# Local attention on one core: transposed product with the values, probabilities scaled by VectorE and GpSimd

## The reference, cut to what matters

```python
qkv = shift_token(x) @ wqkv                  # 128 -> 3 x 512
q, k = l2norm(q) * qs, l2norm(k) * ksc       # per head
q, k = rotary_xpos(q, k)
sim = einsum('bhwid,bhwjd->bhwij', 8.0 * bq, look_around(bk))   # 64 x 128 per window
attn = softmax(where(mask, -max, sim))
x = x + (attn @ look_around(bv)) @ wo
h = layer_norm(shift_token(x)) * lg + lb
a, g = split(h @ w1 + b1)                    # 341 each
x = x + (a * gelu(g)) @ w2 + b2
```

## Time and profile before

| | us |
|---|---|
| runs: median (lowest to highest of 3) | 1923.7 (1919.97 to 1941.29) |
| profiled execution: its own time | 1931.87 |
| profiled execution: span | 1930.0 |
| stage windows(0), tiles in flight | about 330 to 720 |
| stage windows(1), tiles in flight | about 1075 to 1475 |
| TensorE busy in the span | 1632.6 |

### The profile page before, as it was taken

How to read it: one execution, slowest core, us unless ns; L and a number is a source line. 1 busy time by engine, 2 the same in 40 slices (tenths; PEclk the granted TensorE clock), 3 DMA queues, 4 the chain that set the end, 5 groups by cost and what they waited for, 6 DMA issues and landing times. The chain is left out here.

```text
span 1930.0 us, 38058 instructions
## 1 busy us (share of the span) xinstructions
PE 1632.6 (85%) x13334; PEld 1162.4 (60%) x13334; DVE 1219.7 (63%) x3746; ACT 1071.4 (56%) x2763; POOL 905.9 (47%) x668
## 2 busy tenths in 40 slices
PE   5999996899999977899888689999976675959777
PEld 4999995566666643344555366666654554637655
DVE  3555554887777754555754688777745985646465
ACT  3655553778888834566433478888862112325332
POOL 1333333776667612223443677666623674441044
PEclk9999998999999986889756799999998896979889
DMA  5000000111111100000000011111100001110012
GB/s 208 1 1 1 1 1 4 29 33 26 32 27 26 26 6 1 1 1 1 2 1 1 20 29 26 33 28 26 32 15 1 1 1 33 23 33 1 15 30 23
DMA packets 41082, 38.64 MB, mean 20 GB/s; under 512 B 21944, under 2 KB 32192, under 8 KB 40512
## 3 DMA queue, kind: packets, MB, share of 16 engines
q1 hardware_dynamic: 35264, 32.02, 6.4%
q0 software_dynamic: 5632, 4.20, 1.8%
HBM read 13.14 MB, written 4.20 MB: 9 GB/s over the span
## 5 line engine op out<-in xcount | busy, mean ns | idle before, releaser
L979 ACT ACTIVATE arena<-ps 128x512 f32<-128x512 f32 (+5 forms) x680 | 358.2, 581 | 301.1 <-PE ps L327 98.4
L1218 ACT ACTIVATE arena<-ps 128x320 f32<-128x320 f32 (+4 forms) x256 | 131.9, 561 | 153.3 <-PE ps L686 152.3
L1135 ACT ACTIVATE arena<-arena,g_small 128x128 f32<-128x128 f32 x512 | 198.7, 406 | 0.5
L2194 POOL TENSOR_TENSOR arena<-arena,consts 128x512 f32<-128x512 f32 (+1 forms) x64 | 93.0, 1454 | 209.8 <-ACT arena L1218 209.8
L1676 DVE CUSTOM_DVE_ANT_0 arena<-ps,consts,g_ss 128x128 f32<-128x128 f32 x512 | 145.6, 347 | 58.5 <-PE ps L521 58.5
L2234 POOL TENSOR_TENSOR arena<-arena 128x512 f32<-128x512 f32 x64 | 81.9, 1280 | 176.1 <-DVE arena L1684 176.1
L686 PE MATMUL ps<-arena 32*128 32x160 f32 (+4 forms) x1024 | 129.6, 505 | 18.8 <-ACT arena L1218 9.0
L327 PE MATMUL ps<-consts,arena 128*128 128x128 f32 x400 | 81.7, 341 | 59.6 <-DVE arena L1651 11.3
L686 PEld LDWEIGHTS ps<-arena 32*128 32x128 f32 x1024 | 65.8, 232 | 91.4 <-ACT arena L1218 51.9
L1683 DVE TENSOR_TENSOR arena<-ps,tabs 128x512 f32<-128x512 f32 x128 | 87.8, 686 | 52.3 <-ACT arena L1104 45.6
L327 PEld LDWEIGHTS ps<-consts,arena 128*128 128x128 f32 x400 | 55.2, 172 | 100.3 <-DVE arena L1474 20.4
(11 more groups left out here) (257 smaller groups left out, 4180.2 us busy)
## 6 DMA issues: line engine op xcount, KB each, us to landing
arena<-arena SPq DMA_DIRECT2D x112, 128.0 KB, 2.3
weights<-in_w SPq DMA_DIRECT2D x1, 5069.0 KB, 24.3
weights<-in_w SPq DMA_DIRECT2D x1, 2052.0 KB, 12.8
arena<-Y SPq DMA_DIRECT2D x64, 32.0 KB
arena<-Y SPq DMA_DIRECT2D x64, 31.8 KB
consts<-in_c SPq DMA_DIRECT2D x1, 1278.0 KB, 8.7
sorted_rows<-X SPq DMA_DIRECT2D x1, 1024.0 KB, 5.1
X<-sorted_rows SPq DMA_DIRECT2D x4, 256.0 KB, 3.9
```

Of the source, the lines that this page charges most:

```text
L979: copy = lambda o, i: act.activation(o, i, ACT.Copy)
L1135: last = act.activation(g_p[:, n % 2, 4 * hf + i, :], g_sc[:, 4 * hf + i, :], ACT.Exp, scale=-1.0, bias=g_mn[:, h:h + 1], accum_out=g_rs[: ...
L1218: act.activation(b_p[:, U % 2, 2 * gp:2 * gp + 2, at:at + n], ps[:, b:b + 2, 0:n], ACT.Exp, scale=float(HD) ** -0.5).then_inc(s.b_exp, 1)
L2194: pool.tensor_tensor(v, v, m.unsqueeze(1).broadcast_to([P, NG, n]), ALU.mult)\
```

## The change

- `values`: the operands change places. The values are stationary, the transposed probabilities move, and the result comes out transposed (rows are head columns). `turn_out`, its semaphore and the buffer `g_os` go; `keep_out` copies bank 3 instead of bank 2, at the start of the step instead of after `keep_qk`.
- The division by the sums moves ahead of the transposes: VectorE scales the four even heads' probabilities in place (`scale_even`, last in step n), GpSimd the four odd heads' (`scale_odd`, in step n of its loop between the keys' scaling and the queries' root, released by a reciprocal that VectorE makes in step n+1 between the two halves of `minima`). `turn_probs` waits for these instead of for `exps`.
- TensorE's order in a step: `out_rows` where `turn_out` was; `project_v` before `values`.
- VectorE's order: `add_out` between `rope_k` and `rope_q`; `mid` before `sums`; statistics of the feed-forward part at lag 6 instead of 7. `root4(1)` on GpSimd at lag 6 too.
- ScalarE: `gelu` at lag 10 after `keep_qk`, not at lag 9 at the step's end.
- SyncE: `shift(t - 2)` before `lookback(t + 2)`.

```diff
@@ -558,7 +557,7 @@
         N = n0 + n
-        pe.wait_ge(gs.exp, 2 * N + hf + 1)
+        pe.wait_ge(gs.odd if hf else gs.even, N + 1)
         pe.wait_ge(gs.kin if hf else gs.qin, n0 + tiles_by(t + 1))
@@ -572,36 +571,30 @@
         pe.wait_ge(vx_sem[j], (32 if j else 16) * (N // NT + 1))
-        need(pe, gs.os, N)
+        need(pe, gs.oin, N)
         need(pe, gs.hin, m0 + groups_by(t, -3))
         need(pe, gs.y, m0 + groups_by(t, 12))
-        for h in range(HF):
+        for i in range(4):
             for r in range(2):
-                src = g_v if r else g_vx
-                last = mm(ps[64 * r:64 * r + 64, 3, h * DF:(h + 1) * DF],
-                          g_pT[:, 4 * (h % 2) + h // 2, 64 * r:64 * r + 64],
-                          src[:, j, h * DF:(h + 1) * DF], start=True, stop=True, skip_group_check=True)
+                for hf in range(2):
+                    h, src = 2 * i + hf, g_v if r else g_vx
+                    last = mm(ps[64 * hf:64 * hf + 64, 3, i * P + 64 * r:i * P + 64 * r + 64],
+                              src[:, j, h * DF:(h + 1) * DF], g_pT[:, 4 * hf + i, 64 * r:64 * r + 64],
+                              start=True, stop=True, skip_group_check=True)
         last.then_inc(gs.pv, 1)
-
-    def turn_out(n):
-        N = n0 + n
-        pe.wait_ge(gs.os, N + 1)
-        pe.wait_ge(gs.vin, n0 + tiles_by(n + 3))
-        need(pe, gs.add, N)
-        for c in range(4):
-            last = tr(ps[:, 2, c * P:(c + 1) * P], g_os[:, c * P:(c + 1) * P], ident)
-        last.then_inc(gs.ot, 1)
...
         pe.wait_ge(gs.oin, N + 1)
+        pe.wait_ge(gs.vin, n0 + tiles_by(n + 3))
+        need(pe, gs.add, N)
         for c in range(4):
...
     def turn_y(g, t):
-        need(pe, gs.os, n0 + tiles_by(t - 2))
+        need(pe, gs.oin, n0 + tiles_by(t - 2))
         need(pe, gs.hin, m0 + g)
@@ -645,7 +638,7 @@
         if live(t - 2):
-            turn_out(t - 2)
+            out_rows(t - 2)
         if at_step(t, 10):
@@ -659,12 +652,10 @@
                 up((t - lag) // 4, c, half, t)
-        if live(t - 2):
-            out_rows(t - 2)
+        if live(t + 2):
+            project_v(t + 2, t)
         if live(t - 1):
             values(t - 1, t)
-        if live(t + 2):
-            project_v(t + 2, t)
         if at_step(t, 7):
@@ -1122,9 +1113,9 @@
         N = n0 + n
-        act.wait_ge(gs.ot, N + 1)
+        act.wait_ge(gs.pv, N + 1)
         need(act, gs.out, N)
-        copy(g_oT, ps[:, 2, :].rearrange("p (c t) -> p c t", c=4)).then_inc(gs.oin, 1)
+        copy(g_oT, ps[:, 3, :].rearrange("p (c t) -> p c t", c=4)).then_inc(gs.oin, 1)
@@ -1171,12 +1162,14 @@
     for t in range(-4, TILES + 9):
+        if live(t - 2):
+            keep_out(t - 2)
         if live(t + 2):
...
             keep_qk(t + 1)
-        if live(t - 2):
-            keep_out(t - 2)
+        if at_step(t, 10):
+            gelu((t - 10) // 4)
         if live(t - 1):
@@ -1193,8 +1186,6 @@
             keep_hn((t - 7) // 4)
-        if at_step(t, 9):
-            gelu((t - 9) // 4)
         for i in {34: (1, 3), 36: (7,), 39: (13,)}.get(t, ()) if F == 0 else ():
@@ -1659,12 +1650,22 @@
     heads = lambda t: t.rearrange("p (h d) -> p h d", h=HF)
-
-    def norm_out(n):
+    halves = lambda t: t.rearrange("p (i f) -> p f i", f=2)
+
+    def reciprocals(n, hf):
         N = n0 + n
-        dve.wait_ge(gs.pv, N + 1)
-        need(dve, gs.ot, N)
-        tt(heads(g_os), heads(ps[:, 3, :]), wide(g_ri, [P, HF, DF], 2), ALU.mult).then_inc(gs.os, 1)
+        ri, rs = halves(g_ri)[:, hf, :], halves(g_rs[:, n % 2, :])[:, hf, :]
+        dve.wait_ge(gs.exp, 2 * N + hf + 1)
+        if hf:
+            need(dve, gs.odd, N)
+            dve.reciprocal(ri, rs).then_inc(gs.odd_ri, 1)
+        else:
+            need(dve, gs.even, N)
+            after(dve.reciprocal(ri, rs), True)
+
+    def scale_even(n):
+        probs = g_p[:, n % 2, 0:4, :]
+        tt(probs, probs, wide(halves(g_ri)[:, 0, :], [P, 4, P], 2), ALU.mult).then_inc(gs.even, 1)
@@ -1728,49 +1723,44 @@
     for t in range(-4, TILES + 9):
-        first, group = (t + 4) // 4, (t - 7) // 4
+        first, group = (t + 4) // 4, (t - 6) // 4
         fresh = at_step(t, -4) and first < NB
...
             norm_stats(0, x)
-        if at_step(t, 7):
+        if live(t):
+            minima(t, 0)
+        if live(t - 1):
+            reciprocals(t - 1, 1)
+        if fresh:
+            norm_var(0)
+        if live(t):
+            minima(t, 1)
+        if at_step(t, 6):
             dve.wait_ge(gs.sh, 176 * (m0 + group + 1))
             norm_stats(1, g_h)
-        if live(t):
-            minima(t, 0)
-        if fresh:
-            norm_var(0)
-        if at_step(t, 7):
             norm_var(1)
-        if live(t):
-            minima(t, 1)
         if live(t + 2):
             rope_k(t + 2)
+        if live(t - 2):
+            add_out(t - 2)
         if fresh:
...
             rope_q(t + 2)
-        if live(t - 2) and at_step(t, 10):
-            add_out(t - 2)
-        if live(t + 2):
-            sums(t + 2)
-        if live(t - 2) and not at_step(t, 10) and not at_step(t, 12):
-            add_out(t - 2)
+        for lag, half, c in FFN_STEPS:
+            if half == 1 and at_step(t, lag):
+                mid((t - lag) // 4, c)
         if at_step(t, 7):
...
             norm_apply(1, g_hn, g_h, gs.h2)
-        if live(t - 1):
-            reciprocals(t - 1)
+        if live(t + 2):
+            sums(t + 2)
+        if live(t):
+            reciprocals(t, 0)
+            scale_even(t)
         if at_step(t, 12):
             add_down((t - 12) // 4)
-        if live(t - 2) and at_step(t, 12) and not at_step(t, 10):
-            add_out(t - 2)
-        for lag, half, c in FFN_STEPS:
-            if half == 1 and at_step(t, lag):
-                mid((t - lag) // 4, c)
-        if live(t - 1):
-            dve.wait_ge(gs.dve_step, stepped.n)
-            norm_out(t - 1)
         if F == 0 and t == TILES + 1:
@@ -2237,13 +2227,16 @@
-    def roots(n):
+    def roots_k(n):
         N = n0 + n
...
                            ss[:, 8:16].unsqueeze(2).broadcast_to([P, HF, DF]), ALU.mult).then_inc(gs.ka, 1)
+
+    def roots_q(n):
+        ss = g_ss[:, n % 2, :]
         pool.tensor_tensor(ss[:, 0:8], ss[:, 0:8], C("neghalf", 0, 8), ALU.pow).then_inc(gs.root, 1)
@@ -2258,6 +2251,13 @@
+    def scale_odd(n):
+        probs = g_p[:, n % 2, 4:8, :]
+        ri = g_ri.rearrange("p (i f) -> p f i", f=2)[:, 1, :]
+        pool.wait_ge(gs.odd_ri, n0 + n + 1)
+        pool.tensor_tensor(probs, probs, ri.unsqueeze(2).broadcast_to([P, 4, P]), ALU.mult)\
+            .then_inc(gs.odd, 1)
+
     stepped_after(pool.memset(g_vx[0:64, 0, :], 0.0))
@@ -2269,11 +2269,15 @@
             root4(0)
-        if at_step(t, 7):
+        if at_step(t, 6):
             root4(1)
...
             turn_pairs(t + 2)
-            roots(t + 2)
+            roots_k(t + 2)
+        if live(t):
+            scale_odd(t)
+        if live(t + 2):
+            roots_q(t + 2)
         if at_step(t, 8):
@@ -2429,10 +2433,10 @@
     for t in range(-4, TILES + 9):
+        if live(t - 2):
+            shift(t - 2)
         if live(t + 2):
             lookback(t + 2)
-        if live(t - 2):
-            shift(t - 2)
```

10 lines of the change are left out of this document (2 added, 8 removed).

## The result

The changed kernel took 1913.21 us (median of 10 runs, 1909.86 to 1920.58) against 1922.52 us for the kernel before (10 runs on the same chip). The medians are 9.3 us apart; the ratio, 0.9937 [0.9915, 0.9959], makes it about 12 us. The forecast was 1900 us and 0.9876, that is 24 us less. The direction was right and the gain about half of the forecast. The gain lies within the 1% that the forecast called no change, and 1913.2 us lies just past the slow end of its own 1888 to 1912, inside the whole range of 1876 to 1927. The profiled execution has a span of 1909.0 us.

The account below looks back on a forecast made before the run. TensorE was taken to set the pace. Steady cycles 14 us, attention-only and first steps 9, last two tiles 1: 24 us off, 1907.9 profiled, or 1900 by the same ratio on the median; range 1876 to 1927.

Parts of the forecast that it names:

- attention step: Step of local attention alone, between starts of score products: from 9.02 to 8.3 us, with TensorE's floor at 7.95.
- A: First step of the four-tile steady cycle in the window stages: 9.3 us forecast, 9.79 before, TensorE's floor 9.27.
- GpSimd's 8.3: GpSimd's work per tile with scale_odd and gaps, taken as the longest term and so the attention-only step's length.
- B: Second, crowded step of the cycle, with two up products, mid and gelu: 9.8 us forecast, 11.54 before.
- D: Fourth step of the cycle, holding down, with late keys: 12.8 us forecast, 12.71 before.
- Step C: Third step of the cycle: 0.7 us wait for g_oT, h2 0.4 to 1.1 late; 10.75 forecast, 10.01 before.
- The stage's start and its tail I leave as they are: Both ends of each window stage assumed unchanged; a change above 3 us was a sign of being wrong.
- last two tiles: 1: Term of the sum for the last two tiles: 1 us gained.
- rival 1: Cover holds: delays in the second and third steps are absorbed, TensorE stays the bound; 49 us gained, 1875 us; chance 0.20.
- rival 3: VectorE becomes the bound because scale_even meets GpSimd additions or products; cycle near 47 us, 1950 us; chance 0.10.
- Rival 4: Removed transposes become TensorE idle time because the keys' chain sets every step; 1918 to 1924 us; 0.25 with rival 2.
- Rival 2: GpSimd's root holds the ports, so scale_even waits and delays the keys; gain 3 us, 1921 us; 0.25 with rival 4.

Follow-up runs that it names:

- experiment 8: Changed kernel with ScalarE's gate copy (lag 9) ahead of the exponentials: 1907.63 us, ratio 0.9902 to the kernel before.
- experiment 9: Changed kernel with add_bias ahead of scale_odd on GpSimd: 1897.13 us, ratio 0.9868 to the kernel before.
- experiment 10: Changed kernel with both the gate copy ahead of the exponentials and add_bias ahead of scale_odd: 1900.97 us, ratio 0.989 to the kernel before.
- Experiment 6: Changed kernel with the shifted rows issued behind the look-back again, statistics still at lag 6: 1945.76 us, ratio 1.0104 to the kernel before.
- Experiments 2: Changed kernel with gelu, mid, statistics, root4 and shift put back, normalisation still ahead of the sums: 2009.3 us, ratio 1.0469 to the kernel before.
- experiment 3: Changed kernel with gelu back at lag 9 at the step's end and mid last on VectorE: 1992.89 us, ratio 1.037 to the kernel before.
- 4: Changed kernel with only gelu back at lag 9, mid still ahead of the sums: 1922.58 us, ratio 0.9972 to the kernel before.
- experiment 7: Changed kernel with scale_odd moved from GpSimd to VectorE: 1913.47 us, ratio 0.9944 to the kernel before.
- experiment 1: Kernel before with gelu, mid, normalisation, statistics, root4 and shift moved as in the change, without the new product and division: 1943.32 us, ratio 1.0117.
- 12: Changed kernel with gate copy and add_bias moved earlier, and the last up ahead of the probabilities' transposes: 1897.24 us, ratio 0.9834 to the kernel before.

## Why the prediction was right or wrong

- **TensorE sets the pace: right.** The page, the air in 40 us and the cycle say it again. TensorE's floor lies 0.3 a step lower than I reckoned: an attention step runs without a wait at 7.65 us (my floor was 7.95), and A without its wait takes 8.82 (experiment 8), where I had 9.27. I had counted the removed transposes alone. From start to start in A, the value projection now takes 0.95 in place of 1.23 (it takes 1.05 in step D of the same cycle, so nearly 0.2 was the wait for the gate copy, which I had left in A's floor), `out_rows` 0.89 in place of 0.99 and the probabilities' transposes 0.88 in place of 0.95. With the 0.52 of the turn that is 0.97, and 9.79 less 0.97 is 8.82. Why products of the same shape follow closer in the new order wasn't tested.
- **"GpSimd's 8.3 is then the longest: I take 8.3": wrong by 0.65.** GpSimd's work per tile is what was forecast, and in the step of 364.14 its round (from one keys' root to the next, 364.67 to 372.74) took 8.07 us with hardly a gap. But TensorE's step took 7.65 at the same time, without a wait. Only a few such steps follow each other; that GpSimd goes into them with slack enough to cover 0.4 us a step is my reading, which no run tests. If it holds, the sum of an engine's work sets the pace only where it lasts longer than the slack in front of it.
- **Steps B and D: right.** B 9.62 (9.8), without a wait for `mid`; D 12.29 (12.8). "Step C 10.75": 10.91. The normalised rows came late as said (0.54, forecast 0.4 to 1.1). The 0.7 for `g_oT` is hardly there; in its place TensorE stands 0.26 for the keys and 0.33 ahead of the probabilities' transposes. So the size of C was right, and one of its two terms.
- **"Step A: 9.3": wrong, 10.06.** I listed who comes late when TensorE gets faster and left out the gate copy behind the exponentials, which set this step already before the change (0.26 us ahead of the scores in both kernels), so that taking work from TensorE could not by itself shorten it. Experiment 8 shows it: that one line moved brings A to 8.82. Why the copy comes 0.27 us later than before was not looked into. It came 0.76 above the forecast, and B (0.18 below) and D (0.51 below) hid that in the sum of 42.88.
- **"The stage's start and its tail I leave as they are" and "last two tiles: 1": this step failed, and with it the size.** The sum by segments: t 10 to 30 gave 6.8 and 6.7 (forecast 7 each), t 2 to 10 gave 4.2 and 3.9 (forecast 4.5 each), together 21.6 of the forecast 23. Given back were 1.8 and 3.2 in the last attention step and 1.6 and 4.2 in the tail, 10.8 in all, where I had +1. That the second tail grew by more than 3 us was my own sign of being wrong. The keys behind `add_bias` are shown by experiment 9 (8.30 in place of 12.32). The tails differ between kernels with the same code there: 61.7 to 65.8 us in the change and in experiments 8 to 10. Their waits nearly agree, the copy behind the last exponentials (2.79) among them, but for the same products TensorE is busy 40.4 and 38.3 us in the tails of experiment 10, and 43.8 and 41.0 in those of experiment 9, at granted clocks of 0.88 and 0.85 against 0.84 and 0.79. So a part of what I called given back in the tail is clock, 1.6 us of the 4.2 in its last `down` alone. How much of it the change brings about by its own waits stays open.
- **"The shifted rows: worth nothing by itself": true as said, and misleading.** Experiment 6 prices the place at 13 us a stage, by the wait that I had named as the sign.
- **The parts don't add.** I costed each edit against the kernel before. Experiments 2 to 4 show that `scale_even` turns an unneeded move into a needed one: it waits for the exponentials at the end of VectorE's step, and all behind it waits too. With `mid` ahead the price is nothing; with `mid` behind it and `gelu` at lag 9 it is 7.1 us a cycle, of which 2.6 are TensorE's slower clock behind the wait. I had placed `mid` rightly in the timing of B, but not seen that it stood between us and a rival at 2009 us.
- **The rivals.** The cover didn't hold (rival 1; the cycle is 42.88, not 40.55). VectorE wasn't the bound (rival 3): `scale_even` was 0.77 in the mean. Its sum was also off: 36 + 5.3 + 0.9 + 4 is 46.2 and not 47, so its cycle would have been 2.2 us worse and not 3. Rival 4 is refuted by the cycle. Rival 2's premise is answered below.

## The ports

Root on GpSimd and `scale_even` on VectorE at once, in order of time after:

```profile
581.89 1.65 POOL L2234 TENSOR_TENSOR g_ss<-g_ss,consts 128x8 f32<-128x8 f32 x1 [2.27 <-DVE g_ss L1707]
...
581.93 0.71 DVE L1668 TENSOR_TENSOR arena<-arena,g_small 128x512 f32<-128x512 f32 x1
```

A running root didn't block a VectorE product of two SBUF tensors: 0.71 us. Starts that lie 0.04 us apart prove little by themselves, but 53 of the 64 `scale_even` began 0.03 to 1.32 us behind the start of a root that was running, and all of them took 0.69 to 0.71 us and the roots 1.64 to 1.66. That is what the forecast took from the scalings of the earlier trace rows, and rival 2's premise falls. In step A above it went the other ways: the product that began at 602.74 during GpSimd's addition ran until 604.09, 0.55 after the addition's end at 603.54, and the root that began at 603.50, while that product ran, took 2.09 in place of 1.65. All six roots that began during such a product took 2.09 to 2.17. The clamp of 16 columns (L1707) took 1.30 beside the addition of 600.93; its mean rose from 0.35 to 0.53, and falls to 0.26 when `scale_odd` leaves GpSimd (experiment 7). The Trainium skill (SBUF — State Buffer, SBUF: two separate sides) makes the shared port pair an exclusive lock held for the whole instruction by whichever starts first. The trace agrees for additions on GpSimd and for the root that came second, and disagrees for the root that came first.

## What to carry to other kernels

When an instruction that waits for a slow engine is put at the end of an in-order queue, look at everything queued behind it: here one such product cost nothing or 7 us on a cycle of 43, by the place of one other. Price a wait of the pacing engine with what may follow it: here 4.24 us of standing were followed by 2.6 us lost to the slower clock, each time. When the pacing engine gets faster, list every consumer it meets, once for the steady cycle and once for the stage's end, since what a cycle hides comes out there; here half of the gain was given back in the last two tiles. Test the parts of a change in combinations and read them by segments between recurring instructions, not by the span, when another stage's clock moves it by more than the change does. Before two medians of a few executions are compared, look at the granted clocks of those executions.

## What was not expected of the hardware

A GpSimd power of eight columns doesn't hold back a VectorE product that starts beside it (0.71 us), but is held back itself by one already running (2.09 in place of 1.65). A one-input VectorE operation of 16 columns can take 1.30 us in place of 0.17 beside a GpSimd addition. After TensorE had stood 4.24 us, it worked 5.48 us at a granted clock of 0.50, in each of the ten cycles of experiment 3. After 1.95 us the scores ran slow (1.98 in place of 1.10) in four of the ten cycles of experiment 1. After the 1.16 us in step A of the change nothing of the kind is seen between tiles 10 and 30 (1.00). And the same code between the two window stages took 321 us in one execution and 306 in the other, at granted clocks of 0.76 and 0.84.

What stays open: step C at 10.9 with all edits; an earlier normalisation, which would tell whether C reaches TensorE's 9.33, was not tried. The medians of experiments 9, 10 and 12 don't follow the order of their window stages (801.1, 788.1, 796.7); they go with the clocks that their executions happened to get, and what decides those wasn't looked into.
